# Attention values of four heads in one burst of matmuls, and a new order of the last steps of each half batch

## The reference

```
q = rope((x @ wq).reshape(B, N, 32, 8)); k = rope((x @ wk).reshape(B, N, 8, 8)); v = (x @ wv).reshape(B, N, 8, 8)
k, v = repeat(k, 4, axis=2), repeat(v, 4, axis=2)
scores = einsum('bhqd,bhkd->bhqk', q, k) / sqrt(8)
scores = where(causal, scores, -inf)
weight = softmax(scores, axis=-1)
out = einsum('bhqk,bhkd->bhqd', weight, v).reshape(B, N, 256) @ wo
```

## Time and profile before

| | us |
|---|---|
| median of 3 runs | 1050.88 |
| lowest and highest | 1050.41, 1057.42 |
| the profiled execution's own time | 1054.82 |
| its span in the trace | 1053.0 |
| the second attention's half batches in it, i = 0 to 7, from scoresT(i, 0) to scoresT(i+1, 0) | 26.39, 18.48, 26.87, 18.38, 27.83, 18.38, 22.85, 14.66 |

### The profile page before, as it was taken

The page is one execution under the profiler, slowest core; times in us unless marked ns, Lnnn a source line. Parts: engine busy times, 40 slices in busy tenths (PEclk is TensorE's granted clock), DMA queues, the critical chain, the costliest instruction groups (busy, mean ns, idle before and its releaser), DMA issues.

```text
span 1053.0 us, 18249 instructions
## 1 busy us (share of the span) xinstructions
PE 913.4 (87%) x6216; PEld 656.6 (62%) x6216; DVE 797.4 (76%) x2089; ACT 572.9 (54%) x1458; POOL 191.2 (18%) x168
## 2 busy tenths in 40 slices
PE   2989988988898889679999999788898998899993
PEld 1777676867686777454566666523333437788983
DVE  7689889988988899984299996557666766366664
ACT  2698489838973798241233332246474761555551
POOL 1102030103001301037344443200000005011111
PEclk9999999989999999779999999969998987799997
DMA  9999950000000000035467784424464544788773
GB/s 247 199 204 237 239 141 1 2 1 1 1 2 1 1 1 2 1 124 177 133 204 242 237 250 135 173 81 164 178 218 160 210 174 138 268 324 295 275 271 130
DMA packets 71452, 153.80 MB, mean 146 GB/s; under 512 B 11439, under 2 KB 53054, under 8 KB 67136
## 3 DMA queue, kind: packets, MB, share of 16 engines
q1 hardware_dynamic: 65696, 139.93, 44.2%
q0 software_dynamic: 5664, 12.71, 3.3%
HBM read 122.09 MB, written 62.19 MB: 175 GB/s over the span
## 4 chain that ended last, share of the span: by engine, by line
PE 53%; DVE 25%; ACT 8%; DMA 6%; issue 5%; POOL 1%; SPq 1%; DVEq 0%; ACTq 0%; POOLq 0%
PE ps L1796 48%; DVE arena L1546 2%; DVE arena L1209 2%; DMA arena<-slots 2%; DVE arena L1199 2%; DVE arena L1226 2%; DMA arena<-split 2%; ACT arena L693 2%; POOL slots L582 1%; ACT arena L659 1%; ACT arena L686 1%; DMA made<-arena 1%; DVE arena L1179 1%; DVE arena L1775 1%; DVE den L1040 1%
## 5 line engine op out<-in xcount | busy, mean ns | idle before, releaser
L1796 PE MATMUL ps<-arena 128*128 128x128 f32 (+15 forms) x4652 | 711.4, 333 | 39.8 <-DVE arena L1199 16.2
L1796 PEld LDWEIGHTS ps<-arena 128*128 128x128 f32 (+7 forms) x4652 | 489.2, 149 | 189.1 <-issue 88.0
L1546 DVE TENSOR_REDUCE arena<-ps 128x4 f16<-128x1024 f32 (+1 forms) x48 | 58.8, 1227 | 52.5 <-PE ps L1796 52.5
L1226 DVE SCALAR_TENSOR_TENSOR arena<-arena 128x128 f32<-128x128 f32 x240 | 91.8, 442 | 0.4
L1773 DVE CAST arena<-arena 128x128 f16<-128x128 f32 (+1 forms) x128 | 33.2, 259 | 62.9 <-ACT arena L919 60.3
L659 ACT ACTIVATE arena<-ident,arena 128x128 f32<-128x128 f32 x256 | 80.2, 392 | 0.0
L824 ACT ACTIVATE arena<-ps 128x1024 f32<-128x1024 f32 x48 | 49.2, 1025 | 45.6 <-PE ps L1796 45.5
L919 ACT ACTIVATE arena<-ps,arena 128x128 f32<-128x128 f32 (+1 forms) x128 | 50.1, 417 | 44.0 <-PE ps L1796 38.8
L562 POOL DMA_INDIRECT made<-arena x47 | 53.0, 1128 | 87.0 <-DVE arena L1459 85.5
L528 POOL TENSOR_TENSOR den<-den,backd 128x512 f32<-128x512 f32 x8 | 11.9, 1482 | 280.7 <-DVE euv L1021 232.6
L1040 DVE RECIPROCAL den<-den 128x128 f32<-128x128 f32 x64 | 57.6, 928 | 0.4
(11 more groups left out here) (301 smaller groups left out, 1234.0 us busy)
## 6 DMA issues: line engine op xcount, KB each, us to landing
arena<-split SPq DMA_DIRECT2D x15, 2048.0 KB, 9.8
arena<-in_w0all SPq DMA_DIRECT2D x32, 608.0 KB, 4.5
slots<-in_blank SPq DMA_DIRECT2D x17, 1040.0 KB, 18.7
arena<-in_w1all SPq DMA_DIRECT2D x16, 1024.0 KB, 6.9
split<-arena SPq DMA_DIRECT2D x32, 512.0 KB, 3.1
slots<-in_blank SPq DMA_DIRECT2D x10, 1044.0 KB, 23.0
arena<-slots SPq DMA_DIRECT2D x47, 130.0 KB, 3.1
side<-made SPq DMA_DIRECT2D x8, 512.0 KB, 5.7
```

The source lines that it names most:

```text
L1226: ins = dve.scalar_tensor_tensor(dst, prob[:, n % 3, tiles[tt]], w, dst, ALU.mult, ALU.add)
L1546: dve.tensor_reduce(out, ps[:, at:at + 2].rearrange("p j (r s) -> p j r s", r=nr), X, ALU.max, negate=True).then_inc(max1_done, 1)
L1796: return pe.matmul(o, l, r, start=start, stop=stop, skip_group_check=shared)
```

## The change

In `scoresT` the step is read the other way round: k = 0 and 1 are the first kind for the first and the second pair of heads, 2 and 3 the second kind, 4 and 5 the third. So after every second step one kind is there for all four heads. `values(i, kind)` is now called three times per half batch instead of six, and does four heads in the four column groups, one after the other: eight records of 512 columns for the first two kinds, sixteen of 256 columns for the third. The semaphore `pv1_pe` counts to three per half batch instead of six. The number of matmuls and their columns stay as they were.

The order changes too. values(i, 0) stands in step 3 behind scores(i+1, 3), values(i, 1) in step 5, and values(i, 2) behind turn_maxed(i+1). In step 5, scores(i+1, 5) comes ahead of scoresT(i, 5).

```diff
@@ exps1 (ScalarE)
                 if u >= 4:
-                    act.wait_ge(pv1_pe, u - 3)
+                    act.wait_ge(pv1_pe, (u - 4) // 2 + 1)
@@ outputs_out (ScalarE)
-                act.wait_ge(pv1_pe, 6 * i + 6)
+                act.wait_ge(pv1_pe, 3 * i + 3)
@@ scoresT (TensorE)
-                jp, kind = divmod(k, 3)
+                kind, jp = divmod(k, 2)
@@ values (TensorE)
-            def values(i, k):
+            def values(i, kind):
 
                 b, half = divmod(i, 2)
-                jp, kind = divmod(k, 3)
-                u = 6 * i + k
-                pe.wait_ge(exp1_done, u + 1)
-                if k == 0 and i:
+                pe.wait_ge(exp1_done, 6 * i + 2 * kind + 2)
+                if kind == 0 and i:
                     pe.wait_ge(oraw_read, i)
                 for rp in ((kind,) if kind < 2 else (0, 1)):
-                    for j in range(2):
-                        g = 2 * jp + j
-                        o, p = ps[32 * g:32 * g + 32, 4 + rp], probT1[:, u % 4, j]
+                    for g in range(4):
+                        o, p = ps[32 * g:32 * g + 32, 4 + rp], probT1[:, (6 * i + 2 * kind + g // 2) % 4, g % 2]
@@ the loop over half batches (TensorE)
                 for k in range(6):
+                    if more and k == 5:
+                        scores(i + 1, k)
                     scoresT(i, k)
-                    if more:
+                    if more and k < 5:
                         scores(i + 1, k)
-                    if k:
-                        values(i, k - 1)
+                    if k in (3, 5):
+                        values(i, k // 2 - 1)
@@
                 if more:
                     turn_maxed(i + 1)
-                values(i, 5)
+                values(i, 2)
```

## The result

| us | before | after |
|---|---|---|
| median of 17 runs each | 1053.30 | 1062.77 |
| lowest and highest | 1050.18, 1057.42 | 1055.70, 1070.01 |
| span of the profiled execution | 1053.0 | 1061.0 |

The ratio after to before is 1.0088, 95% interval 1.0069 to 1.0107: slower by some 9 us, where 2.3 us of gain were forecast. The time, 1062.77, lies above the range of 1043 to 1055. The runs also spread twice as far, 14 us instead of 7.

The account below looks back on a forecast made before the run. It took three engine loops as nearly level in odd half batches and VectorE as holding the second half of even ones, despite TensorE's 87%. 2.0 - 0.6 + 0.4 + 0.5 = 2.3 us off 1050.88 gave 1048.5, range 1043 to 1055.

Parts of the forecast that it names:

- Four heads at once: Bursts of values: four heads take the 0.99 us of two, saving 2.97 us of TensorE per half batch, 23.8 for eight.
- the 20 that were given as a sign: Sign in the profile after: TensorE's busy time falls by some 20 us while the span does not.
- the groups do not run together: Rival: a four-head burst costs 1.98 us, TensorE saves nothing, about 1 us lost per half batch, 1059; chance 0.03.
- The odd i: Half batches i = 1, 3, 5: of 2.97 us taken from TensorE in each, 0.67 us arrive as gain.
- Three such half batches: 2.0 us: Sum for i = 1, 3 and 5, each gaining 0.67 us.
- the clock falls where it did not: Rival: new pauses halve the odd i's clock, 1.9 us for each of three, 5.7 in all, time 1055; chance 0.12.
- The trace supports it only at pauses above 2 us in this loop: Reason for the clock rival's chance of 0.12: in this loop only pauses above 2 us support a fall of the clock.
- The even i: Half batches i = 0, 2, 4 with rotate: bursts gain, the swapped order loses; sum -1.2 us, at full clock +2.1.
- the tail: Even i, restart in step 5 to turn_stacks: 6.3 us, 7.4 at lower clock, after a pause of about 4.0 us.
- I take -0.6: Value taken for i = 0, 2 and 4 together, between -1.2 at half clock and +2.1 at full clock.
- i = 6: Half batch 6: two bursts gone ahead of routing, step 5 pushes turn_maxed back; gain 0.4 us, bounds -0.3 and 1.8.
- i = 7: Last half batch, without scores: the second old burst was on the chain; gain 0.5 us, bounds 0 and 1.1.

Follow-up runs that it names:

- filler bursts: Changed kernel plus useless two-head bursts of values in steps 1, 2 and 4 of each half batch: ratio to before 1.0062.
- values alone: Changed kernel with the old order in step 5 (scoresT, then scores), four-head bursts kept: ratios to before 0.9972, 0.9951 and 0.9974.
- the changed kernel with the chunk earlier: Changed kernel with the last chunk of the weights' splitting done in step 4 instead of step 5: ratio to before 1.0052.
- order alone: Kernel before with scores(i+1, 5) ahead of scoresT(i, 5), its six two-head bursts kept: ratio to before 1.0055.
- the second profile: Changed kernel unaltered, measured and profiled once more beside the third set's other kernels: ratio to before 1.0119.
- the pair of repeated kernels: Changed kernel, and the same with the old order in step 5, both measured again: ratios to before 1.0119 and 0.9951.
- the third set: Set with two mask-filled kernels (0.9998; kernel before with masks 1.0017), the changed kernel again (1.0119) and its old-order version again (0.9951), ratios to before.
- the bursts one step earlier: Changed kernel with the old order in step 5 and values(i, 0) and values(i, 1) in steps 2 and 4 instead of 3 and 5: ratio to before 1.0090.
- values(i, 1) behind turn_maxed: Changed kernel with the old order in step 5 and values(i, 1) moved from ahead of turn_maxed(i+1) to behind it: ratio to before 1.0097.
- the filled pause: Changed kernel plus useless mask matmuls ahead of scores(i+1, 5), twelve in even half batches, four in odd: ratio to before 1.0115.
- old order with pause and bursts: Changed kernel, old order in step 5, eight masks in the even i's pause, useless two-head bursts in steps 1 and 2 of odd i: ratio to before 0.9991.
- filling the rest as well: Old order with pause and bursts, plus four masks ahead of turn_stacks and three ahead of the odd i's first scores: ratio to before 0.9998.
- values alone with the chunk earlier: Changed kernel with the old order in step 5 and the last chunk of the weights' splitting moved to step 4: ratio to before 0.9997.
- before with pauses filled: Kernel before plus masks ahead of turn_stacks, the odd i's first scores, and four in its pause before step 5: ratio to before 1.0017.

## Why the prediction was wrong, point by point

**Four heads at once: right.** In the changed kernel sixteen records of 256 columns over four column groups took 1.07 us (718.70), where the prediction had 0.99. The same columns for two heads took as long in the kernel before, in this row:

```profile
781.31 1.06 PE L1796 MATMUL ps<-arena 128*32 128x256 f32 x8
```

TensorE's busy time in the stage fell from 157.5 to 148.2 us although more of it ran at half clock; over the page it fell by 10.2 us, not by the 20 that were given as a sign. The rival that the groups do not run together is out.

**The odd i: the arithmetic right, the clock wrong.** Where an odd half batch kept its clock, it went as computed. In i = 5 the scores of step 5 restarted 13.66 us after the start of the half batch (forecast 13.48, before 14.57), and the 2.50 us from there to turn_maxed are the computed 0.65 + 0.86 + 0.99. It gained 0.45 for 0.67. The step that failed is "Three such half batches: 2.0 us", which took for granted the 1.00 that the clock had in all of them before. Instead of +2.0 they brought -4.5: i = 1 lost 4.22, i = 3 0.73. The rival *the clock falls where it did not* named the place and the sign, but priced it at 1.9 us per half batch, and i = 1 ran at half clock for 13.7 us, which made it 4.9 us longer than the forecast 17.8. Its chance of 0.12 rested on "The trace supports it only at pauses above 2 us in this loop". That reading was wrong for the kernel before already. In its i = 6, whose 0.93 stands in the earlier trace rows, the clock fell at 844.36 with TensorE busy for 16.84 of the 17.06 us before and no single wait above 0.22 us:

```profile
827.30:844.36 17.06, 16.84 (x130) 8.75 (x129) 11.33 (x22) 11.13 (x15) 0.00 (x0) 1.00 0.69 243
844.36:847.77 3.41, 3.41 (x11) 0.48 (x10) 2.30 (x5) 1.45 (x3) 0.00 (x0) 0.50 0.05 19
```

The trace of after has the fall in i = 1 behind waits of 0.93 us at most, the last 0.46 (727.63), and in i = 3 behind one of 1.33 us:

```profile
785.11 0.39 PE L1796 MATMUL ps<-causal,identb 128*128 128x256 bf16 x2 [1.33 <-DVE arena L1546]
...
788.22 0.77 PEld L2189 LDWEIGHTS ps<-ident,arena 128*128 128x128 f16 x8 [1.44 <-issue]
```

The masks at 785.11 still took 0.39; from 787.0 the clock was half, and the eight transposes' loads took 0.77 where they take 0.45. But the same wait in i = 5 left the clock at full:

```profile
831.82 0.39 PE L1796 MATMUL ps<-causal,identb 128*128 128x256 bf16 x2 [1.33 <-DVE arena L1546]
...
834.31 0.45 PEld L2189 LDWEIGHTS ps<-ident,arena 128*128 128x128 f16 x8 [0.84 <-DVE arena L1546]
```

The waits of 0.47 and 0.46 us stand in i = 3 and 5 as well, and the clock stayed full behind them. So no length of one wait decides it. What had changed in all of the odd i is that TensorE had less work between its waits: it was busy 14.07 of 17.96 us in i = 5, and 16.79 of 18.38 in i = 3 before. That this lost the clock is supported by the filler bursts, which put the work back and ran every odd i at 1.00. It is not the whole rule: values alone, with the same thinner odd i, kept the clock in i = 1 and 3 and lost it in i = 5, in all three of its profiles. The Trainium skill, in "TensorE: Matmul & The Clock Gate", section "HAM oscillation — how this bites in real kernels", describes a loop of bursts of about 2 us, with waits of some 3 to 5 us for a DMA between them, that loses the clock in each round. No wait in the odd i of after is longer than 1.33 us, so this is not the page's case; the clock fell here behind shorter waits, and the measurement decides.

**The even i: right in the tail, wrong in i = 0.** 7.41 us for 7.4, 6.34 at full clock for 6.3, pause 3.94 for 4.0. i = 2 and 4 came to +0.82 and -0.38 for +0.8 and +0.2. But i = 0 lost 2.19 where 2.1 gained and 2.3 lost were set against each other. Values alone shows which half of this was missing: its i = 0 is 26.49, 0.15 *longer* than before, at 0.64 instead of 0.77. The two bursts that were to give 2.1 us gave nothing, and the half clock with which the stage begins lasted 12.0 us into it (to 703.8) where it had lasted 8.5 (to 701.0); in the changed kernel it was 12.3. "I take -0.6", between -1.2 and +2.1, was worked out with the clock of before in i = 0; the measured sum, -2.6, lies outside both bounds.

**i = 6: the clock again.** +0.4 was forecast, between -0.3 and 1.8; it lost 1.82. TensorE is busy nearly throughout there (22.63 of 22.85), so its length goes with the clock: 20.77 and 21.72 at 1.00 (the changed kernel with the chunk earlier, order alone), 22.85 at 0.93, 24.67 at 0.79. The half clock stood from 848.4 to 858.6, right behind the routing matmuls, though no run shows that they caused it:

```profile
846.97 2.27 PE L1796 MATMUL ps<-arena 128*128 128x8 f32 x16 [0.37 <-DVE arena L1098]
```

Neither bound has a term for a lower clock. i = 7 gave 0.75 for 0.5, and 1.7 of loss in the second profile, at 0.69.

**The sum.** Of the 10.5 us between the forecast of +2.3 and the -8.2, 6.5 are in the odd i, 2.2 in i = 6, and 2.0 in the even i with rotate. i = 7 was 0.25 better. All the large errors are terms where the clock of before was carried over into a kernel with less TensorE work between its waits. (1050.88 less 2.3 is 1048.6, not 1048.5.)

**What the change was.** The bursts alone are a small gain, by 0.28, 0.49 and 0.26% in three measurements (the interval of the third just takes in no change), 3 to 5 us. The windows don't show where it sits: each profile of values alone is of the slowest execution of its set (1053.97, 1070.11 and 1074.01 us, with medians of 1051.36, 1062.64 and 1065.30), and its stage is 174.2 to 174.4 us where before has 173.9. The swap in step 5 turns the gain into a loss: 1.30 us in each even i at full clock, 1.5 to 2.4 as measured in the pair of repeated kernels (26.54, 26.20, 25.70 to 28.94, 27.65, 27.67), 0.4 to 0.7 in an odd one. On the old values the swap cost 0.55%; on the new ones it cost 1.2% (1.0088 against 0.9972) and, in the third set, 1.7% (1.0119 against 0.9951). In the profiles the extra part sits in the odd i, where the swap was free on the old values, and in i = 6 and 7: there order alone ran at 1.00 where before ran at 0.93 and 0.88, and it so won back 2.3 us of its price.

**What stays open.** Why one pattern of bursts and waits loses the clock and the next keeps it was not settled: values alone, the bursts one step earlier and values(i, 1) behind turn_maxed have the same matmuls, and odd windows of 17.5, 21.2 and 19.9. Filling some of the waits moved the half clock elsewhere (24.5 us in the odd i of the filled pause); old order with pause and bursts removed more than half of it (25.6 us left of 59.8), and filling the rest as well removed no more (26.4). And one profile per kernel can't rank kernels that are 4 us apart: values alone with the chunk earlier has the shortest stage of all, 170.9 us, and a median no better than before. The best kernel found is values alone, the new bursts with the old order in step 5, at 0.9951 to 0.9974 of before; against the changed kernel its lead is clear, against before it is near the limit of what can be measured.

## What to carry to other kernels

Taking work from a busy engine pays only in the stretches where that engine ends last. On TensorE it also thins the work between waits, and here the granted clock then fell in half batches that had kept it (i = 1 and 3): price the half clock over the whole stretch, for every part that ran at full clock before. When an instruction is moved ahead of another, follow what the second one feeds over all engines; here a swap of 0.65 against 0.86 us of TensorE made a chain over three engines 1.3 us longer. And split a change of two parts before you judge it: this one is a small gain and a larger loss.

## What the runs showed of the hardware

- Four heads in four column groups take as long as two in two: 16 records of 256 columns 1.07 us (after, 718.70), 8 records of 256 columns for two heads 1.06 us (before, 781.31), for twice the sums.
- The granted clock fell to half behind waits of 0.93 us and less in one half batch of after (i = 1), stayed full behind one of 1.33 us in another (i = 5) and fell behind the same 1.33 us in a third (i = 3). In i = 6 of before it fell at 844.36 with no wait above 0.22 us in the 17 us ahead of it. The stretches at half clock were 3.4 to 20.5 us long.
- Half clock is not lost time by itself: the kernel with the lowest ratio had 59.8 us of it in this stage, and before with pauses filled had 12.4 and was no faster than before.
- Of values alone on two chips the eight windows agreed within 0.05 us, yet the spans were 1052.2 and 1068.3 us (on a third within 0.14, span 1072.2); of the changed kernel, single windows differed by up to 3.6 us.
